# Repeated matmuls of TensorE in eleven of its waits

## The reference

```python
x = _layernorm(x + L0_attn(x))           # attention, 4 query groups x 8 heads, key width 8, plus a linear memory
x = _layernorm(x + L0_xattn(x, ctx))     # rotary cross attention, 8 heads, softmax over 256 channels
x = _layernorm(x + L0_ffn(x))            # 8 experts of width 1024, top 2 of them per token
x = _layernorm(x + L1_attn(x))           # 16 heads; values come from a triangular solve in chunks
x = _layernorm(x + L1_xattn(x, ctx, m))  # masked cross attention, 16 heads
x = _layernorm(x + L1_ffn(x))            # 64 experts folded into 8 shared ones with low-rank mixes, plus a shared MLP
```

## Time and profile before

| | |
|---|---|
| three timed runs | 1102.22, 1103.02, 1108.24 us; median 1103.02 |
| the profiled execution | 1100.47 us, span 1098.6 us |
| mean granted clock of TensorE | 0.932 |
| TensorE busy | 972.1 us (88%) |
| VectorE busy | 553.1 us (50%) |
| ScalarE, GpSimd busy | 362.9 us, 200.3 us |
| the chain that ended last | TensorE 71%, VectorE 20%, issue 3%, ScalarE 2%, DMA 2% |

### The profile page before, as it was taken

How to read it: one execution, slowest core, us unless ns; L and a number is a source line. 1 busy time by engine, 2 the same in 40 slices (tenths; PEclk the granted TensorE clock), 3 DMA queues, 4 the chain that set the end, 5 groups by cost and what they waited for, 6 DMA issues and landing times.

```text
span 1098.6 us, 18957 instructions
## 1 busy us (share of the span) xinstructions
PE 972.1 (88%) x7488; PEld 610.9 (56%) x7488; DVE 553.1 (50%) x1114; ACT 362.9 (33%) x726; POOL 200.3 (18%) x241
## 2 busy tenths in 40 slices
PE   7998879998899999993964799998699999999995
PEld 4765523333468899981443367757565444444443
DVE  2599788895431111015578676545854333233324
ACT  3434346766222223321367255043231000000002
POOL 5020100000012222210025841032000111111110
PEclk9999869999799999996987799998879999999998
DMA  6000000000745455523000202030014122222101
GB/s 237 2 2 1 1 1 2 2 2 1 278 144 179 150 188 185 169 89 121 1 1 1 77 2 97 1 137 3 1 48 93 41 87 88 88 75 72 29 1 38
DMA packets 27242, 75.15 MB, mean 68 GB/s; under 512 B 9860, under 2 KB 17292, under 8 KB 21780
## 3 DMA queue, kind: packets, MB, share of 16 engines
q1 hardware_dynamic: 24948, 67.91, 18.5%
q0 software_dynamic: 2208, 6.03, 2.0%
HBM read 67.48 MB, written 6.46 MB: 67 GB/s over the span
## 4 chain that ended last, share of the span: by engine, by line
PE 71%; DVE 20%; issue 3%; ACT 2%; DMA 2%; POOL 0%; SPq 0%; DVEq 0%; ACTq 0%; POOLq 0%
PE psum L1523 8%; PE psum L1098 8%; PE psum L1110 7%; DVE arena L2090 4%; PE psum L821 3%; PE psum L1527 3%; PE psum L1289 3%; PE psum L1553 3%; PE psum L1511 3%; PE psum L1557 2%; PE psum L1002 2%; DVE arena L2009 2%; DVE arena L2008 2%; PE psum L1548 2%; PE psum L1259 2%
## 5 line engine op out<-in xcount | busy, mean ns | idle before, releaser
L1952 ACT ACTIVATE arena<-psum 128x512 f32<-128x512 f32 (+1 forms) x32 | 19.0, 593 | 220.0 <-PE psum L1527 220.0
L1523 PE MATMUL psum<-arena 128*128 128x512 f32 (+1 forms) x192 | 90.6, 608 | 0.5 <-DVE arena L2565 0.5
L1767 ACT ACTIVATE arena<-psum,arena 128x128 f32<-128x128 f32 x184 | 52.6, 368 | 115.4 <-PE psum L1098 115.4
L2090 DVE TENSOR_REDUCE arena<-psum 128x2 f32<-128x512 f32 x128 | 82.6, 687 | 11.9 <-PE psum L948 9.8
L1098 PE MATMUL psum<-arena 128*128 128x128 f32 x736 | 86.7, 276 | 0.0
L1098 PEld LDWEIGHTS psum<-arena 128*128 128x128 f32 x736 | 84.0, 192 | 2.7 <-issue 2.7
L747 POOL TENSOR_TENSOR arena<-arena 128x512 f32<-128x512 f32 (+1 forms) x32 | 40.5, 1264 | 235.4 <-ACT arena L1952 235.4
L1110 PE MATMUL psum<-arena 128*128 x368 | 83.1, 379 | 0.0
L2237 DVE COPY arena<-psum 128x256 f32<-128x256 f32 x23 | 9.8, 425 | 136.3 <-PE psum L1083 85.9
L1744 ACT ACTIVATE arena<-psum 128x1024 f32<-128x1024 f32 x64 | 65.4, 1024 | 30.9 <-PE psum L970 27.7
L1110 PEld LDWEIGHTS psum<-arena 128*128 128x128 f32 x368 | 68.2, 190 | 8.4
(11 more groups left out here) (370 smaller groups left out, 1826.1 us busy)
## 6 DMA issues: line engine op xcount, KB each, us to landing
arena<-in_w SPq DMA_DIRECT2D x31, 1024.0 KB, 4.9
arena<-in_experts SPq DMA_DIRECT2D x8, 1248.0 KB, 6.1
arena<-mixed SPq DMA_DIRECT2D x16, 256.0 KB
arena<-mixed SPq DMA_DIRECT2D x8, 512.0 KB, 9.3
arena<-in_ctx SPq DMA_DIRECT2D x2, 1024.0 KB, 7.1
arena<-returned SPq DMA_DIRECT2D x8, 256.0 KB, 4.7
arena<-in_w_xattn SPq DMA_DIRECT2D x1, 1538.5 KB, 10.2
arena<-in_w_ffn SPq DMA_DIRECT2D x1, 1152.0 KB, 5.5
```

What stands on the lines that cost most here:

```text
L1523: pe.matmul(out, e[w][:, k, :], xe6[:, half, k, :], start=(k == 0), stop=False)
L1767: last = act.activation(hidt[:, r % 2, ic * P:(ic + 1) * P], bank(n)[:, i * P:(i + 1) * P], ACT.Gelu, bias=b1_tile[:, r % 4, ic:ic + 1])
L2090: ax_max.by(dve.tensor_reduce(nmx[:, b % 2, :, h], bank(u % 2).rearrange("p (t s) -> p t s", t=2), AX.X, ALU.max, negate=True))
```

## The change

A new helper issues matmuls of the identity (the stationary operand) with itself repeated four times (512 columns) into a bank whose contents nobody needs at that point. It waits on nothing and signals nothing. It is called at eleven places of TensorE's list, with `ident` (f32) unless a bf16 copy is named. The program's other engines are unchanged.

```diff
+            def keep_clock(count, spare, eye=ident):
+
+                for _ in range(count):
+                    pe.matmul(bank(spare), eye, wide(eye, 1, BANK // P), start=True, stop=True)
...
                 if b >= 3 and b % 2 == 1:
                     turn_out0(b // 2 - 1)
+            keep_clock(4, 3)
...
                 if u < 2 * NT:
                     project(u)
+                if u == NT + 1:
+                    keep_clock(1, 3)
                 if u > NT:
                     replicate(u - 1)
+            keep_clock(3, 3)
             pe.wait_ge(st_ready.sem, 4 * NT)
             pe.wait_ge(selm_ready.sem, 2)
             for u in range(2 * LEAD):
                 for tc in range(2):
                     first_scores_x(u, tc)
+                keep_clock(1, 5, ident16)
...
                         values_x(b - 1, 1, 0)
+                    if b == B and p >= 1:
+                        keep_clock(2, 5, ident16)
...
+            keep_clock(2, 5)
             turn_x(1)
...
+            keep_clock(8, 0)
             for j in range(NT + 1):
                 if j < NT:
                     turn_heads1(j)
                 if j >= 1:
                     keys_by_keys(j - 1)
+            keep_clock(3, 6)
             for g in range(2):
                 turn_diagonal(g)
...
                 scores1(w)
+                if w == 0:
+                    keep_clock(16, 5)
                 if w >= 1:
+                    keep_clock(2, 5, ident1)
                     turn_probs1(w - 1)
...
                     turn_out5(j - 1)
+                if j == NT + 1:
+                    keep_clock(3, 5)
                 if j >= 2:
                     out5(j - 2)
...
             pe.wait_ge(loaded["w_ffn1"].sem, 16)
+            keep_clock(6, 5)
             for half in (range(0, 4), range(4, NT)):
                 turn_x(4, half)
```

## The result

The change took 1096.7 us, the median of 13 runs (1090.6 to 1100.9), against 1102.4 for the kernel before (13 runs). The ratio is 0.9941 with a 95% interval of 0.9921 to 0.9962: faster by 6.5 us, give or take 2.3. One of the 13 runs before, 1122.3 us, was slow as a whole and is not counted in the ratio. The forecast was 1090 us in a range of 1082 to 1102: the direction and the range hold, but of the 13.4 us of the sum about half came. (The diff has twelve calls of `keep_clock`, not eleven; they are the seven sites of the prediction.)

A forecast was written before the change was run, and what follows sets the result against it. The prediction took the kernel as bound by TensorE between waits, and by VectorE and a DMA at the waits. Seven gains summed to 13.4 us, giving 1090 us, with an 80% range of 1082 to 1102.

The forecast's parts named there:

- Price of a repeat: All sites: an f32 repeat takes 0.86 us at 2.4 GHz (0.43 per record), costing nothing if shorter than its wait.
- The second rival: All sites: the clock ignores the repeats, which run at 1.2 GHz and end late; 1124 us, slower; chance 0.08.
- Site 1: Before `project(NT)` and the first `replicate`: five f32 repeats keep the clock up for the work behind; gain 2.2 us.
- Site 2: First cross scores: three f32 repeats, then one bf16 per head for 14 heads; faster values behind; gain 1.5 us.
- Site 3: Last batch and before `turn_x(1)`: six bf16 and two f32 repeats speed up the router's L1119; gain 3.0 us.
- Site 4: Eight repeats in the 7.9 us wait for VectorE's L2307 speed up the work behind; gain 2.6 us.
- Site 5: Three repeats in the 3.3 us wait before `turn_diagonal` speed up its transposes, partly paced by ScalarE; gain 1.8 us.
- Site 6: Sixteen repeats in the 15.9 us wait for L2327, two bf16 before each of three turns; gain 1.8 us.
- Site 7: Three and six repeats around `turn_x(4)`; clock expected to fall again before the router; gain 0.5 us, bracket -4.6 to 5.
- The sum: The gains of the seven sites add, being in series: 13.4 us.
- The first rival: The clock falls again at thin places and gains may become waits on ScalarE; half the sum, 1097 us; chance 0.22.

The follow-up runs named there:

- 32 repeats: The change with 32 instead of 16 repeats in the long wait for VectorE's masked scores in the second attention: ratio 1.0053 to the kernel before, median 1109.3 us.
- sites 4 to 7 alone: The change with only the repeats of Site 4 to Site 7, those of the first three sites removed: ratio 0.9964 to the kernel before, 4.0 us.
- sites 1 to 3 alone: The change with only the repeats of Site 1 to Site 3, those of the later sites removed: ratio 0.9949 to the kernel before, 5.6 us.
- the thick `turn_x(4)`: The change with 7 instead of 6 repeats before `turn_x(4)` and one more before each of its tiles 2 and 3: ratio 0.9862 to the kernel before.
- the repeats as transposes: The change with each f32 repeat issued as eight 128-column transposes of the identity, each bf16 one as four: ratio 0.9924 to the kernel before.
- all waits filled: The change with the thick `turn_x(4)`, 22 repeats before `turn_x(2)`, 18 instead of 16, and one or two in further waits: ratio 0.9852, median 1086.2 us.

## Why the prediction was half right

- **Price of a repeat, and that it hides in a wait:** right. 0.43 us per record, the waits end after the repeats, and no work of VectorE or ScalarE grew (VectorE's busy time is 553.1 before and 553.2 after). What exceeds a wait is paid in full (32 repeats). The second rival (the clock does not heed repeats) is refuted, for matmuls and for transposes of the identity.
- **Site 1, 2.2:** right, 4.72 - 2.64 = 2.1.
- **Site 2, 1.5:** mis-sized, and not told from nothing by the timed runs. The step that failed is that one bf16 repeat per head holds the clock over the heads and the values behind. The price of a head was too low as well: with its repeat it takes TensorE 0.64 us at the high clock (139.52 to 140.16 in the change) and 1.07 at the low one, not 0.41 and 0.82. So TensorE was not idle for a third of each head, as the prediction feared, and the clock fell all the same. Of nine profiles with one repeat per head, the clock fell in five at 147 to 152 us for 10 us, in two at 153 or 154 for 3.4, and in two not at all; in the four without, it fell at 143 to 145 for 17 to 20. From the first head to the router the nine took 138.3 to 143.4 us, 140.5 on average, the four 138.5 to 142.7, 141.2 on average: 0.7 us, in a spread of 5, in which the falls further on come and go.
- **Site 3, 3.0:** the mechanism was right. 6.19 became 3.70 in the profile of the change; but the repeats end before the transposes, and the wait for w_route behind them was left open. Of the twelve profiles with these repeats, TensorE waits there for 2.0 to 3.0 us in six, and L1132 takes 5.4 us in five of these and 6.1 in the sixth, the change run again; in the six with a wait of 0.4 to 1.3 us it takes 3.7 in five and 5.3 in one (two of the six have one more repeat in this wait). So the gain goes with the wait for the load of w_route, which the prediction named only as something to hide behind; no run changes that wait alone. Without the repeats L1119 took 6.19 and, in the kernel with sites 4 to 7 alone, 4.67. From the router's first record to the first `up` the two profiles without this site's repeats took 37.1 and 37.2 us; the twelve with them 34.5 to 37.9, 35.9 on average: 1.2 us.
- **Site 4, 2.6:** mis-sized. First to last `turn_heads1` took 18.0 us before and 16.5 in every profile that has the repeats: 1.5. The fourth turn is late for VectorE next, as this row of the change shows:

```profile
566.12 0.87 PE L1213 MATMUL psum<-arena 128*128 128x128 f32 x6 [1.14 <-DVE arena L2328]
```

- **Site 5, 1.8:** mis-sized. From the last `turn_heads1` to the first `scores1` 14.65 us became 13.81, 0.8. ScalarE's eight copies of the banks set the pace, which the prediction named and priced at too little.
- **Site 6, 1.8:** failed as a step. From the first L1271 to L1304 it took 27.53 us before and 27.54 after. The prediction priced a path from VectorE to TensorE and back, but the fourth scores, from which L1304 follows, also need the second product of GpSimd's L695, and that comes when GpSimd's part of the inverse and its L717 are done. Before, GpSimd's products began at 615.27, each 1.0 us:

```profile
615.27 10.05 POOL L695 TENSOR_TENSOR arena<-arena 128x512 f32<-128x512 f32 x10
```

The second was done at 617.3, and the fourth scores started at 617.78: there was less than 0.5 us to gain, and the trace of before could tell. The change took it (25.62 us from the first to the fourth scores became 25.24, released by L695) and gave it back with the last pair of bf16 repeats. Even with no repeats at this site (sites 1 to 3 alone) GpSimd released these scores:

```profile
618.38 0.61 PE L1269 MATMUL psum<-arena 128*128 128x512 bf16 x1 [0.87 <-POOL arena L695]
```

The first wait of the change kept 2.7 us unfilled, at the end of which the clock fell for 3.4 us. Without the repeats (sites 1 to 3 alone) the whole stretch took 28.8 us, in the kernels with the sixteen 27.5 to 28.5, so they may be worth up to a microsecond that the trace of before did not show as lost.

- **Site 7, 0.5:** right for the change and for the reason given, thin work behind the repeats. The up to 5 us of the bracket were there for three more repeats.
- **The sum:** the terms as measured, averages where several profiles differ, are 2.1 + 0.7 + 1.2 + 1.5 + 0.8 + 0 + 0 = 6.3 us, and the timed difference is 6.5 give or take 2.3. That they meet so closely is partly luck: the terms of sites 2 and 3 are averages in spreads of 5 and 3 us. The 7.3 us between the two profiles are made up otherwise: falls at which the change does not aim came and went. From the first `scores5` to `turn_x(4)` 48.2 us became 45.4, because the execution before had a fall at 754 us and that of the change none. Site 7 does not decide this: the kernels without it have 45.5 us (sites 1 to 3 alone) and 50.2, and two kernels with it have 51.2, with falls at 745 and 758; the cross attention gave 3.2 us the other way.
- The first rival (half the sum, 1097 us, the clock falls at thin places, gains turn into waits on other engines) describes what happened better than the forecast did.

Left open: what decides whether the clock falls at the places that the change does not aim at (60, 170 to 270, 685, 716, 754 us). It changes between executions of one program, and no experiment here controlled it. The 13 runs of the change spread over 10 us, and their time goes with the mean granted clock: 1099.2 and 1100.9 us at 0.957 and 0.958, 1090.6 and 1091.2 at 0.973 and 0.974. Open too is why the kernel with 22 repeats before `turn_x(2)` is 4 to 5 us faster than the change, and why its fill adds nothing on top of the thick `turn_x(4)`.

## What to carry to other kernels

A wait in front of TensorE's work costs twice: the wait, and the work behind it at 1.2 GHz. Repeats that fit into the wait take the second part away, but only if the work behind is itself dense, or is made dense with a repeat in each of its small waits; three more repeats at `turn_x(4)` brought 5.4 us, nearly as much as all the others together (shown at this one place). Before pricing a site, look at which engine is late once TensorE is not: at four of the seven sites VectorE, ScalarE or GpSimd came next, and at a fifth (the router) a DMA. The trace of before shows how far behind they are. And where profiles of one program differ by more than a term, take a second profile of before ahead of a sum made from one.

## What the runs showed of the hardware

TensorE shown busy is no promise of the clock. It fell in stretches that the page shows as full: in the window from 140.0 to 156.9 us of the change TensorE is busy 16.50 of 16.90 us, and the mean clock is 0.70; it fell among matmuls on 32 rows with a bf16 repeat between them, and why is not shown. It rose over transposes and held over them (1.00 for 9.8 us with the repeats as transposes). With all waits filled, 28.8 us of the recording are at the lower clock, against 152.5 before, and the time fell by 1.5%, 16 us. That is far less than half of the difference, 62 us: waits lay at the lower clock too, and work that other engines paced.

```profile
140.00:156.90 16.90, 16.50 (x102) 5.08 (x101) 13.59 (x24) 5.01 (x6) 0.00 (x0) 0.70 0.00 1
```
